# Attention on TensorE: V's products in four groups per head pair in place of seven, two of the turned tiles copied by the Vector engine

## The reference

```python
q = einsum('btd,od->bto', x, wq); k = ...; v = ...       # 16 heads of 64
q, k = apply_rotary_emb(q), apply_rotary_emb(k)
scores = einsum('bhid,bhjd->bhij', q, k) * 64 ** -0.5
scores = where(causal, scores, -inf)
probs = softmax(scores)
out = einsum('bhij,bhjd->bhid', probs, v)
x = x + einsum('btd,od->bto', out, wo)
```

## Time and profile before

| what | value |
| --- | --- |
| median of 3 runs | 1323.15 us (1322.53 to 1323.75) |
| the profiled execution, its own time | 1324.65 us |
| its span, first to last instruction | 1322.9 us |
| PE busy | 94% of the span |
| ACT, DVE, POOL busy | 69%, 57%, 34% |
| granted TensorE clock, mean | 0.983 of full speed |
| V's products, first to last (32 pairs) | 167.6 to 1240.8 us: 33.5 us for a pair |

### The profile page before, as it was taken

One profiled execution on the slowest core, in us unless ns is written; L12 is line 12 of the kernel. 1 busy time (PEld: TensorE's weight loads), 2 busy tenths in 40 slices (PEclk: granted clock), 3 DMA queues, 4 the chain that ended last, 5 costly groups with the idle time before them and its releaser, 6 DMA issues. The chain is left out here.

```text
span 1322.9 us, 26897 instructions
## 1 busy us (share of the span) xinstructions
PE 1247.7 (94%) x7456; PEld 869.4 (66%) x7456; DVE 754.2 (57%) x1787; ACT 914.8 (69%) x1946; POOL 444.5 (34%) x288
## 2 busy tenths in 40 slices
PE   5986699999999999999999999999999999999898
PEld 2543566777777677767676767676767676766465
DVE  5574446665556666565656565656565656554354
ACT  3654467777777777777777777777777777777574
POOL 5132443333333333333333333333333333330000
PEclk8997799999999999999999999999999999999999
DMA  7122444454544445454545454545454544431000
GB/s 275 45 95 88 124 104 130 110 134 107 142 106 129 121 110 140 97 146 104 145 105 145 105 145 105 145 105 145 105 144 104 135 107 130 108 84 36 1 29 36
DMA packets 107198, 147.80 MB, mean 112 GB/s; under 512 B 11808, under 2 KB 61344, under 8 KB 107040
## 3 DMA queue, kind: packets, MB, share of 16 engines
q1 hardware_dynamic: 106768, 146.65, 41.8%
q10 hardware_dynamic: 400, 0.79, 0.3%
HBM read 36.24 MB, written 10.49 MB: 35 GB/s over the span
## 5 line engine op out<-in xcount | busy, mean ns | idle before, releaser
L936 DVE CUSTOM_DVE_ANT_0 probs<-wide,tri_mask 128x1024 f32<-128x1024 f32 (+7 forms) x512 | 386.0, 756 | 431.3 <-PE wide L637 424.8
L821 ACT ACTIVATE probs<-probs,neg_max 128x1024 f32<-128x1024 f32 (+7 forms) x512 | 395.6, 774 | 160.8 <-DVE neg_max L936 156.8
L832 ACT ACTIVATE shared_a<-bank 128x512 f32<-128x512 f32 (+2 forms) x640 | 339.6, 548 | 111.6 <-PE bank L653 107.8
L653 PE MATMUL bank<-ident,probs 128*128 128x128 f32 x2304 | 366.0, 278 | 3.5 <-ACT shared_a L832 1.3
L653 PEld LDWEIGHTS bank<-ident,probs 128*128 128x128 f32 x2304 | 266.2, 141 | 153.3 <-issue 108.6
L636 PE MATMUL wide<-k_hh,q_hl 128*128 128x512 f32 (+3 forms) x768 | 292.6, 383 | 5.9 <-DMA k_hh<-parts 2.2
L670 PE MATMUL bank<-shared_a,v_cur 128*64 128x256 f32 (+3 forms) x1792 | 297.2, 453 | 0.0
L637 PE MATMUL wide<-k_low,q_hl 128*128 128x512 f32 (+3 forms) x768 | 257.9, 343 | 0.0
L92 POOL TENSOR_TENSOR rotated<-terms,cross 128x1024 f32<-128x1024 f32 x62 | 147.7, 2383 | 291.0 <-DVE cross L86 282.8
L670 PEld LDWEIGHTS bank<-shared_a,v_cur 128*64 128x64 f32 x1792 | 108.7, 136 | 113.2 <-issue 88.2
L1049 POOL COPY inv_wide<-inv 128x512 f32<-128x512 f32 x64 | 39.1, 611 | 376.0 <-DVE inv L944 343.4
(11 more groups left out here) (114 smaller groups left out, 1323.6 us busy)
## 6 DMA issues: line engine op xcount, KB each, us to landing
q_hl<-parts SPq DMA_DIRECT2D x254, 128.0 KB, 2.8
k_hh<-parts SPq DMA_DIRECT2D x254, 128.0 KB, 2.7
v_cur<-shared_b SPq DMA_DIRECT2D x32, 512.0 KB, 5.8
k_low<-parts SPq DMA_DIRECT2D x63, 256.0 KB, 4.2
xn_cur<-xn_scratch SPq DMA_DIRECT2D x15, 1024.0 KB, 5.8
w_qk<-w_scratch SPq DMA_DIRECT2D x32, 256.0 KB, 3.1
w_scratch<-first_w_parts SPq DMA_DIRECT2D x8, 512.0 KB, 3.1
xn_scratch<-shared_a SPq DMA_DIRECT2D x8, 512.0 KB, 3.1
```

The source lines that it names most:

```text
L653: last = nc.tensor.transpose(ring[at % 2][:, col:col + P], probs[g][:, h, OFFSET[g][r] + j * P:OFFSET[g][r] + (j + 1) * P], ident[:])
L821: nc.scalar.activation(own, own, ACT.Exp, bias=neg_max[g][:, col], scale=-1.0, accum_out=sums[g][:, col]).then_inc(probs_done, 1)
L832: nc.scalar.activation(turned[:, slot, to], ring[at % 2][:, 0:w * len(heads)], ACT.Copy).then_inc(ring_free[at % 2], signals)
L936: nc.vector.tensor_tensor_reduce(out=part_of_probs(g, k), in0=wide_banks[k % 2][:, x0:x1], in1=tri_mask[:, SEQ - (x1 - x0):], scale=1.0, s ...
```

## The change

V's products are taken in two groups per half: first the key blocks 0 and 1 (`SPLIT = 2`), then all that are left. So `times_v` is called 2 + 2 = 4 times per pair. In the list of PE three calls go: the one after `score(p, 1, 6)`, the one after `turn_sums(p, 0)`, and the one after `next_score(7)` at the pair's end. Their products move into later calls that were there already: the one after `turn(p, 1, 3)` now takes blocks 2 to 7 of g = 0, and the one after `turn(p, 0, 3)` of the next pair takes blocks 2 to 5 of g = 1.

Turned tiles live until their group is complete, so each key block of a half has a tile of its own, some in `shared_a` (`turned_mem`) and the rest in a new 128x768 buffer, `turned_more`. The two halves use the same memory: g = 1 may overwrite blocks 0 and 1 after the first group of g = 0, the rest after its second (`read_before`), and likewise g = 0 of the next pair.

The copies of turns 7 and 9 of g = 0 move from ACT to DVE: turn 7 stands there behind the rotation of `ahead(2)` and ahead of `max_of(p, 1, 6)`, turn 9 behind `max_of(p, 1, 7)`.

```diff
-        turned = turned_mem[:].rearrange("p (s c) -> p s c", s=4)
+        turned = [[turned_mem[:, 0:1024], turned_mem[:, 1024:2048]] + [turned_mem[:, 512 * j:512 * (j + 1)] for j in range(4, 8)],
+                  [turned_mem[:, 0:1024], turned_mem[:, 1024:2048], turned_mem[:, 2048:3072], turned_mem[:, 3072:3840]]]
+        turned_more = sb("turned_more", [P, 768])
+        turned = [tiles + [turned_more[:, 0:512], turned_more[:, 512:768]] for tiles in turned]
+        SPLIT = 2
...
+        def read_before(p, g, j):
+            steps = SPLIT if j < SPLIT else KEYS[1 - g]
+            return NK * p + steps if g == 1 else NK * (p - 1) + KEYS[0] + steps
...
-                ats = [at for at, (j, heads) in zip(RING[g], TURNS[g]) if j // 2 == d]
+                keys = range(0, SPLIT) if d == 0 else range(SPLIT, KEYS[g])
+                ats = [at for at, (j, heads) in zip(RING[g], TURNS[g]) if j in keys]
...
-                    times_v(p - 1, i - 1 + u, 1 - u, 1, 2)
+                    times_v(p - 1, i - 1 + u, 1 - u, 1, 1)
...
                 score(p, i, u, 1, 6)
-                times_v(p, i, u, 0, 1)
...
                 turn_sums(p, 0)
-                times_v(p, i, u, 0, 2)
...
                 turn(p, 1, 3)
-                times_v(p, i, u, 0, 3)
+                times_v(p, i, u, 0, 1)
...
                 next_score(7)
-                times_v(p, i, u, 1, 1)
                 ahead_v(3)
...
-                if some(NK * p + KEYS[0] * g + j - 3):
-                    act.wait_ge(out_step, NK * p + KEYS[0] * g + j - 3)
+                read = read_before(p, g, j)
+                if some(read):
+                    act.wait_ge(out_step, read)
...
                 exponential(p, 1, 5)
-                keep_turned(p, u, 0, 7)

                 exponential(p, 1, 6)
                 keep_turned(p, u, 0, 8)
-                keep_turned(p, u, 0, 9)
                 exponential(p, 1, 7)
...
+            def keep_turned(p, u, g, t):
+                j, heads = TURNS[g][t]
+                at, w = RING[g][t], P * len(rows_at(g, j))
+                dve.wait_ge(ring_full, ring_count(p, at))
+                read = read_before(p, g, j)
+                if some(read):
+                    dve.wait_ge(out_step, read)
+                to = slice(heads[0] * w, (heads[-1] + 1) * w)
+                nc.vector.tensor_copy(turned[g][j][:, to], ring[at % 2][:, 0:w * len(heads)]).then_inc(ring_free[at % 2], 1)
...
                 ahead(2)
+                keep_turned(p, u, 0, 7)
                 max_of(p, 1, 6)
                 max_of(p, 1, 7)
+                keep_turned(p, u, 0, 9)
                 ahead(3)
```

More of the change, by code:

```diff
@@ L662, in times_v @@
                         pe.wait_ge(head_done, 2 * p + g)
-                ats = [at for at, (j, heads) in zip(RING[g], TURNS[g]) if j // 2 == d]
+                keys = range(0, SPLIT) if d == 0 else range(SPLIT, KEYS[g])
+                ats = [at for at, (j, heads) in zip(RING[g], TURNS[g]) if j in keys]
                 for b in sorted({at % 2 for at in ats}):
                     pe.wait_ge(ring_free[b], bank_count(p, max(at for at in ats if at % 2 == b)))
-                for j in (2 * d, 2 * d + 1):
+                for j in keys:
                     w = P * len(rows_at(g, j))
-                    slot = (NK * u + KEYS[0] * g + j) % 4
                     for h in range(2):
@@ L671, in times_v @@
                                                 v_cur[:, u, j, HEAD_DIM * h:HEAD_DIM * (h + 1)],
-                                                turned[:, slot, h * w:(h + 1) * w], start=(j == 0), stop=(j == KEYS[g] - 1))
+                                                turned[g][j][:, h * w:(h + 1) * w], start=(j == 0), stop=(j == KEYS[g] - 1))
                     last.then_inc(out_step, 1)
@@ L795, in _ @@
                 pair(ALL_PAIRS // 2 - 1, u, False, True)
-            times_v(ALL_PAIRS - 1, ALL_PAIRS // 2 - 1, 1, 1, 2)
+            times_v(ALL_PAIRS - 1, ALL_PAIRS // 2 - 1, 1, 1, 1)
             project_out(ALL_PAIRS - 1, ALL_PAIRS // 2 - 1, 1, 1, 0, ALL_PAIRS)
@@ L827, in keep_turned @@
                 act.wait_ge(ring_full, ring_count(p, at))
-                if some(NK * p + KEYS[0] * g + j - 3):
-                    act.wait_ge(out_step, NK * p + KEYS[0] * g + j - 3)
-                slot = (NK * u + KEYS[0] * g + j) % 4
+                read = read_before(p, g, j)
+                if some(read):
+                    act.wait_ge(out_step, read)
                 to = slice(heads[0] * w, (heads[-1] + 1) * w)
-                nc.scalar.activation(turned[:, slot, to], ring[at % 2][:, 0:w * len(heads)],
+                nc.scalar.activation(turned[g][j][:, to], ring[at % 2][:, 0:w * len(heads)],
                                      ACT.Copy).then_inc(ring_free[at % 2], signals)
```

## The result

The changed kernel takes **1359.07 us** (median of 4 runs, 1358.95 to 1359.96) against 1322.84 in the same comparison (4 runs, 1321.08 to 1323.75): the ratio is 1.0277, 95% interval 1.0259 to 1.0295, 36 us slower. The profiled execution has a span of 1357.4 us, 34.5 more than before, or 1.08 us per pair.

A forecast was written before the change was run, and what follows sets the result against it. PE was taken to bound the kernel. Two pairs lose 2 x 0.63 + 0.23 + 0.02 = 1.51 us, 0.755 each, 24.2 us in 32, taking the median from 1323.15 to 1347.3 us; range 1327 to 1360.

The forecast's parts named there:

- highest case: Three waits per pair each lay bare 0.10 us of a weight load: 9.6 us more, 1357.
- rival C: Slower still: each wait moves the next, turn 0 of g = 1 waits 0.3 to 0.5 us; 1357 to 1364, chance 0.09.
- Turn 9 and the sums: Turn 9 waits 0.40 us for DVE's copy; `turn_sums` waits 1.07 us for ACT's delayed copy of turn 8.
- From the sums to turn 4: Turn 0 of g = 1 follows without wait; the stretch from turn 7 to turn 4 loses 0.63 us per pair.
- The pair's end: Removing the group behind `next_score(7)` loses 0.23 us with u = 0 at `ahead_v(3)`, 0.02 with u = 1 at turn 1.
- 0.10 of a weight load laid bare: At each of PE's three waits in a pair, a weight load no longer runs beside other work: 9.6 us more.
- A: Faster: no waits, saved changes remain, `turn_sums` by 620.32 or at 619.48; 1286, or 1290 with pair's-end waits; chance 0.12.
- B: No change: turn 8's copy is free 0.6 us earlier, the stretch loses nothing; 1327 or 1323 to 1325, chance 0.05.
- Falls from 342 waits to some 200: Profile sign: idle time of PE or its weight loads before V's products occurs in fewer waits.
- About 1.1 us: Profile sign: new wait before `turn_sums`, released by ACT's copy, about 1.1 us in each pair.
- 0.4: Profile sign: new wait of about 0.4 us before turn 9, released by DVE's copy.
- 0.6: Profile sign: `ahead_v(3)` waits about 0.6 us for ACT in every second pair.

The follow-up runs named there:

- f_pair_end_only: Kernel before with only the pair's end edited: g = 1 in blocks 0-1 and 2-5, g = 0 in its four old groups, copies on ACT; 1330.09 us.
- e_one_group_less: Kernel before with only the V group behind `turn_sums(p, 0)` merged into the next, copies on ACT, the changed kernel's tiles; 1313.98 us, ratio 0.9923.
- j: Changed kernel with both copies on ACT, those of turns 8 and 9 ahead of `exponential(p, 1, 6)`; 1330.65 us, ratio 1.0046.
- i: Kernel before with one V group more: block 0 of g = 0 ahead of `score(p, 1, 4)`, block 1 behind it; 1337.58 us, ratio 1.0111.
- h: `e_one_group_less` with g = 1's group of blocks 2-3 moved from behind `next_score(7)` to ahead of `turn_sums(p, 1)`; 1296.98 us, ratio 0.9796.

## Why the prediction was right, and where it was short

The direction, the places and the causes came out as written. The size did not: the point forecast of 1347.3 gave 24 of the 36 us. The forecast's own highest case was 1357; that 1359.07 lies inside the range, 0.9 us below its edge, is luck, since the room above 1357 was there for rival C, whose mechanism did not come.

- **Turn 9 and the sums.** In the old times turn 9 was put at 618.96 and stands at 618.92; the sums at about 620.95 and stand at 621.01. The DVE copy, taken as 0.68 with 0.61 to the next start, measures 0.68 and starts the maximum 0.59 later. This agrees with the single rate that the Trainium skill names for fp32 out of PSUM (VectorE: DVE Perf Modes, Why PSUM operands drop a tier); the estimate from that page's cycle table was 0.66.
- **From the sums to turn 4: the mis-sized term.** "Turn 0 of g = 1 follows at 621.30" stands at 621.47: 0.06 from the sums and 0.11 from having turn 0 directly behind them (634.56 - 634.10 = 0.46, where I took 0.35). The long group then takes 641.04 - 638.51 = 2.53 where its blocks and the leaving made 2.50. PE enters the group at 625.42 in the old times, 0.17 behind my walk, and turn 4 comes 0.83 late in place of 0.63. That is 6.4 us in 32 pairs.
- **The pair's end.** With u = 0 `ahead_v(3)` starts 1.23 us behind the sums, 603.47 in the old times against 603.46 forecast, but its six products take 0.81 and not 0.72. From turn 4 to the group of block 0 in the next pair: 21.26 us (604.75 to 626.01) against 20.93 (591.99 to 612.92), 0.33 lost where 0.23 were forecast. With u = 1: 18.64 (641.04 to 659.68) against 18.55, 0.09 where 0.02 were forecast; turn 1 comes where it was forecast, and its four transposes take 0.41 in place of 0.35. `f_pair_end_only` confirms it with 6.5 us.
- **Sum.** 2 x 0.83 + 0.33 + 0.09 = 2.08 us per two pairs against 1.51, 33 us of the 34.5 of the span. Of my bounds, the "0.10 of a weight load laid bare" at each wait was nearest, but only in size: behind the waits at the pair's end 0.09 and 0.06 are lost, while of the 0.11 at the sums 0.09 stands in `e_one_group_less` too, without a wait. That the weight loads are the cause is not shown.
- **The rivals.** A and B fall by the wait of 0.95 us at the sums, which stand at 621.01 and not at or before 620.32. j goes further: there the sums start 6.56 us behind the group of block 0, at 619.48, the point that A asks for, and even so the kernel did not gain its 33 us, since the next chain took over. (A's 1290, with waits at the pair's end alone, is a slip in the prediction: 0.83 saved less 0.125 lost per pair is 22.6 us, so 1301.) That the changes have a price is shown by i; that taking them away pays where the cover is kept is shown by e, and that filling a wait pays by h. C named the price that was measured, 1357 to 1364, for another reason: its wait that moves turn 0 of g = 1 did not come, since DVE's second copy is over at 633.38, and turn 0 starts at 634.56.
- **"Falls from 342 waits to some 200"** was wrong. There are 340 idle stretches before V's weight loads, 79.7 us: a long group has short ones between its blocks, which this list counts the same. So the earlier trace rows was no measure of the changes, and its 0.25 us are no sign that changing drains the array; the price per change, taken from the timeline, is the measure. PE's share fell to 91%, near the 92% forecast. "About 1.1 us" at the sums reads 0.95, "0.4" at turn 9 reads 0.20 on PE and 0.52 on its weight loads, "0.6" at `ahead_v(3)` 0.42.

What stays open: how the 0.09 us between four transposes and the four directly behind them arise, and what the 0.06 to 0.09 behind a wait are made of.

## What to carry to other kernels

Work on the bounding engine that stands between a producer and its late consumer is also the cover of the chain that the other engines run meanwhile. Cover means here time in which the others' work is hidden. Before taking it away, measure that chain by rows and compare it with what is left on the bounding engine; where the cover is short, reorder the waiting queue, or move the work to a place where the engine already waits, as h did for 17 us. After one chain is shortened, look for the next one under the same cover, as `ahead(4)` was.

## What the runs showed of the hardware

- Moving between the 128*128 and the 128*64 products costs PE 0.32 to 0.39 us in and out: 0.10 entering from scores or 0.17 from transposes, 0.16 leaving, 0.06 to 0.10 on the first products behind (scores behind plain transposes lose 0.08 of that too). Between the key blocks of one group next to nothing is lost: 24 records of a long group took 2.53 us for 2.34 of products and 0.16 of leaving.
- Four transposes with four others directly behind them, into the other bank, take 0.44 to 0.46 us to that next start in place of 0.35 (e, j and the changed kernel).
- A DVE copy of fp32 from PSUM took 0.68 us for 128x512 and 0.42 for 128x256, with ACT at 0.57 to 0.60 and 0.36 for the same.
